# Mamba's dt bias as a row of ones in the product, softplus in three ScalarE steps, and new orders of turns

## The reference

```python
def mamba_block(x, Wi, cw, cb, Wx, Wdt, bdt, Alog, Dp, Wo):
    xz = x @ Wi.T
    xs, z = jnp.split(xz, 2, axis=-1)          # 256 inner features each
    ...                                        # causal convolution of xs, 4 taps
    u = jax.nn.silu(conv + cb)
    xdbl = u @ Wx.T                            # 8 + 16 + 16 columns
    dt, Bc, Cc = jnp.split(xdbl, [DT_RANK, DT_RANK + D_STATE], axis=-1)
    dt = jax.nn.softplus(dt @ Wdt.T + bdt)
    A = -jnp.exp(Alog)
    # h = exp(dt A) h + dt B u ; y = C h, over 256 steps, 16 states
    y = y + u * Dp
    y = y * jax.nn.silu(z)
    return y @ Wo.T
for i in range(NUM_LAYERS):
    x = mamba_block(layer_norm(x, ln_w[i], ln_b[i]), ...) + x
```

## Time and profile before

| | |
|---|---|
| median of 3 runs | 1870.89 us (1869.44 to 1872.04) |
| the profiled execution | 1878.92 us |
| its span, first to last instruction | 1877.1 us |
| busy: TensorE, VectorE, ScalarE, GpSimd | 80%, 81%, 72%, 63% |
| mean granted clock of TensorE | 0.877 |

### The profile page before, as it was taken

The page is one execution under the profiler, slowest core; times in us unless marked ns, Lnnn a source line. Parts: engine busy times, 40 slices in busy tenths (PEclk is TensorE's granted clock), DMA queues, the critical chain, the costliest instruction groups (busy, mean ns, idle before and its releaser), DMA issues. The chain is left out here.

```text
span 1877.1 us, 27473 instructions
## 1 busy us (share of the span) xinstructions
PE 1493.4 (80%) x9417; PEld 1056.8 (56%) x9417; DVE 1519.8 (81%) x2326; ACT 1342.7 (72%) x2733; POOL 1186.2 (63%) x999
## 2 busy tenths in 40 slices
...
PEclk9677767678899999777799999989999997989998
...
GB/s 191 1 69 74 123 9 92 108 68 92 128 113 119 124 102 108 71 64 23 68 120 130 105 130 137 79 111 46 119 133 137 140 102 69 65 32 79 115 21 6
DMA packets 84585, 170.10 MB, mean 91 GB/s; under 512 B 9440, under 2 KB 14944, under 8 KB 84064
## 3 DMA queue, kind: packets, MB, share of 16 engines
...
## 5 line engine op out<-in xcount | busy, mean ns | idle before, releaser
L1058 POOL TENSOR_TENSOR m<-m 128x1024 f32<-128x1024 f32 x256 | 765.8, 2996 | 191.5 <-DVE m L1049 191.3
L1049 DVE TENSOR_TENSOR_SCAN m<-m,dtuB 128x1024 f32<-128x1024 f32 x256 | 584.4, 2283 | 30.5 <-ACT m L1025 10.6
L1025 ACT ACTIVATE m<-m,Aneg 128x255 f32<-128x255 f32 x1024 | 429.9, 497 | 28.0 <-DMA m<-m 18.4
L1041 DVE TENSOR_TENSOR dtuB<-m 128x1024 f32<-128x1024 f32 x256 | 373.0, 1457 | 9.8 <-DMA m<-m 2.4
L1464 PE MATMUL ps<-o 128*128 128x256 f32 x512 | 151.3, 407 | 24.9 <-DVE X L1408 12.8
L1077 PE MATMUL ps<-m,w_const 128*32 128x256 f32 x2048 | 158.3, 439 | 12.5 <-POOL m L1058 12.5
L1431 ACT ACTIVATE o<-ps,w_mo 128x256 f32<-128x256 f32 x256 | 114.3, 470 | 61.1 <-PE ps L1464 59.7
L364 POOL TENSOR_TENSOR o<-o,mhalf 128x2 f32<-128x2 f32 x64 | 20.5, 320 | 204.9 <-DVE o L358 204.7
L964 PE MATMUL ps<-m,wc 128*128 128x256 f32 x512 | 135.2, 423 | 8.6 <-ACT m L385 8.6
L1472 PE MATMUL ps<-o 128*128 128x128 f32 x1024 | 130.8, 281 | 5.6 <-ACT o L1431 5.5
L1472 PEld LDWEIGHTS ps<-o 128*128 128x128 f32 x1024 | 123.8, 195 | 16.2 <-issue 10.3
...
## 6 DMA issues: line engine op xcount, KB each, us to landing
m<-m SPq DMA_DIRECT2D x256, 256.0 KB, 4.8
...
o<-in_mox SPq DMA_DIRECT2D x128, 256.0 KB, 3.0
...
```

The source lines that it names most:

```text
L1025: op = e.activation(dA[at % NA][:, j, 1:CH], R[q][:, h * CH + 1:h * CH + CH], ACT.Exp, scale=Aneg[:, l, 4 * g + j:4 * g + j + 1])
L1041: e.tensor_tensor(dtuB[:, :, :], bc(R[q][:, (2 + h) * CH:(3 + h) * CH].unsqueeze(1), 4, CH), Br[k % 2], ALU.mult).then_inc(S.dve, n.tick(f ...
L1049: e.tensor_tensor_scan(flat(G[at % NG]), flat(dA[at % NA]), flat(dtuB[:, :, :]), 0.0, ALU.mult, ALU.add).then_inc(S.dve, n.tick(f"s{g}"))
L1058: e.tensor_tensor(G[at % NG], G[at % NG], Cr[k % 2], ALU.mult).then_inc(S.pool, n.tick(f"c{g}"))
```

## The change

The bias of dt goes into the product: W_x gets a 41st column of zeros, so that row 40 of its result is zero; the copy to `v.xd` becomes an Identity step with a bias column that is 1 in row 40 and 0 elsewhere; and row 40 of the W_dt operand holds the bias. The product in PSUM is then v itself. Abs reads it from there, the Ln step writes to SBUF, and VectorE's L858 takes the maximum from PSUM and adds the SBUF part.

```diff
-MB, NMB = cols([("win", 512), ("wx", 2, 40), ("wdt", 256), ("wout", 2, 128),
-                ("cb", 2), ("bdt", 2), ("alog", 8, 4), ("dp", 2), ("lnw", 1), ("lnb", 1)])
+MB, NMB = cols([("win", 512), ("wx", 2, 41), ("wdt", 256), ("wout", 2, 128),
+                ("cb", 2), ("one", 1), ("alog", 8, 4), ("dp", 2), ("lnw", 1), ("lnb", 1)])
...
 ORDER = {
     "sp":
-        "uf3s8f3s8f3s8f3s8f3s8f3s8f3s8f3s8f2sa2s2fs4asa5fafa2s2bsbsbs4f2b2fbfsbs3bs4b3a3f3s2as2as4a4f3s3as2asa2sb3sa3f3sb"
+        "uf3s8f3s8f3s8f3s8f3s8f3s8f3s8f2s4fs4f2sa2s2fs4asa6f2b2asas4fs2bsb3f3s5b2s3b3a3f3s2as4as2a2faf2as4a2sasbsabsba3f3"
...
# Front.dve
-                e.scalar_tensor_tensor(v.dt, v.dt, 0.0, halves_of(b), ALU.max, ALU.add).then_inc(F.dve, n.tick("dt"))
+                e.scalar_tensor_tensor(v.dt, halves_of(b), 0.0, v.dtu, ALU.max, ALU.add).then_inc(F.dve, n.tick("dt"))
...
# Front.act
-                e.copy(v.xd[0:40, :], b[0:40, 0:CH]).then_inc(F.act, n.tick("xd"))
+                e.activation(v.xd[0:41, :], b[0:41, 0:CH], ACT.Identity, bias=m("one", l)[0:41, 0:1]).then_inc(F.act, n.tick("xd"))
                 yield
                 e.wait_ge(F.pe, n.pe("wd"))
-                for h in range(2):
-                    e.activation(v.dt[:, h, :], b[:, h * CH:h * CH + CH], ACT.Identity,
-                                 bias=m("bdt", l)[:, h:h + 1]).then_inc(F.act, n.tick(f"v{h}"))
-                e.wait_ge(F.act, n.act("v1"))
-                e.activation(v.dtu, v.dt, ACT.Abs).then_inc(F.act, n.tick("ab"))
+                e.activation(v.dtu, halves_of(b), ACT.Abs).then_inc(F.act, n.tick("ab"))
...
-                e.activation(halves_of(b), v.dtu, ACT.Ln, bias=1.0).then_inc(F.act, n.tick("ln"))
+                e.activation(v.dtu, v.dtu, ACT.Ln, bias=1.0).then_inc(F.act, n.tick("ln"))
...
# Front.pe
-                    op = e.matmul(b[0:40, 0:CH], m("wx", l)[:, h, :], v.u[:, h, :], start=h == 0, stop=h == 1)
+                    op = e.matmul(b[0:41, 0:CH], m("wx", l)[:, h, :], v.u[:, h, :], start=h == 0, stop=h == 1)
...
-                    op = e.matmul(b[:, h * CH:h * CH + CH], m("wdt", l)[0:40, h * 128:h * 128 + 128], v.xd[0:40, :],
+                    op = e.matmul(b[:, h * CH:h * CH + CH], m("wdt", l)[0:41, h * 128:h * 128 + 128], v.xd[0:41, :],
...
# packing of the weights
-        xs = wx[:, bc + list(range(8))]
+        xs = np.concatenate([wx[:, bc + list(range(8))], np.zeros((256, 1), np.float32)], axis=1)
+        one = np.zeros((128, 1), np.float32)
+        one[40] = 1.0
         wdt[32:40] = g("L1_attn_W_dt")[l].T
+        wdt[40] = g("L1_attn_b_dt")[l]
```

More of the change, by code:

```diff
@@ L214 @@
+        "sbs4b2s3b5f3bsbs3bs4b2f3s8f2sas3fs4f2bs3fs4a3sfafsafs4asas2a4f3s7b3sb3fbf2s3bs5b3a3f2afa2sas6a2sa5b3afaf2s5bs3b7"
+        "f2b2s3bs2bfbs3f3sa4s5a2sa2sa4f3s8b5f3bsbs2bs2asb2s2ba2ba2faf2s5as3a2f3s8a3ba2b2af3b2s6bsasb5f3b2s3bs2bs3bf3s8a12"
+        "b10ab2a10b2ababa2b3ab9ab",
     "pe":
-        "a9ua2ua3ba2ba7bab2ab8ab2ab2ab5a3bab2a2f2b3faf2bab2abasa4b2a3fa2f2af2sa2bab2abab2asb2fab4sfabfsaf2bfsb2fsab2af2af3"
-        "b2sa3bab2a2safbabasa5fafbfa2fsfa6sa2fasaf2b2sfafafb2sb2fa2fsfbf2bfb2sb8sb2afsb4fsf3bfbsfsa2bf3asf2b2asfa2sbababa2"
@@ new lines @@
+        "a9uaua4ba2ba7b2a2b10ababab6a3bab2a2bfbfbf2afasbab3a4b2a5fafaf3sba6b2sbfbab2sb3abfbfbsfaf2b3sbfa2sf2baf2bfb2a2ba2"
+        "sba2sbafa2ba4fafsabf3a2sa3ba4sfa2b2afsfsa2f3bsb2f2a2f2bfsbfsb7sb6fb2sbsf2abf3sbsfba3f2bfbsf2asa3b2fba4bfbfbafaf2"
+        "ba2s2a2b2asbfsa2ba2f2abfa2fbafsa3ba3b2a2sa2babfasbab2f2sabfbfafba3ba5ba2sb2a2bfaba2bsabfafb2fbfsbfb2a2ba2basba2b"
+        "afa6babfa4bfa2fa3fabfbs2bab7ab2sb6abfasbab2a2fbfafsfabfb3sfb4fa2b6fb4fa2fa2fsbsaba2b2a2sabfb2a2b2a3safa2fabf2baf"
+        "asa2b2ababa5ba3sab2afb3afafb2faf2s2b12sb2fb2a3babf2b2fa3safsfab3a2sa2b2fafasbfafaf2asb3aba3sabfba2bsfb2fabfafa2b"
@@ new lines @@
+        "b3a2bab2",
+    "dve":
+        "au2a7ubu3b7a11ba2fb2fb3a7b5fb2fs3fs2bsbs2bs4b2sb2fs8fs2f2as8a2sfafa2fsfs4as4asa2safbs2a2s2b2s3ba2ba2saba2fs2f2s6"
+        "bsb2sb2fs8fs2f2s6as2a2sb2f2a2babsb2fbfbs6bs6fas8fs4f2s7a2f2afasfs2bfs12fsb2a2b3sfsbaf2babafbasbs8bfbs7a2fsbf2sas"
+        "a2sbsabs2bs4fs8fs2as2f2a2sb2s4absb2afsabs3fsaf2s11afsbasfs2bfbafs2abs4as3a2sbfs2abas2asbsa2fsbs3f2s2bs2as2as3afa3"
+        "bfa2f2sas3bs2asbs2asasb2s2a3ba3ba2fabs2b2as2asas3a2fb2f2bsa4sa3fb5sbs5b2fbs3b6sb2abs2fba2fb2fa2fasb2s4ab2sb5fs7a2"
+        "safaf2s2a2s6as2as2bfs2babsabsb2s2fs2f2s2bs5b2sbabfas4b2sa3fsaf2sb4s8fs7faf2a2s3absbas4b2asbsfbas4as4fsfsas2fsabs3"
+        "b2a2bfs2bs2a2sbfa2bsf2as2a2bs4bs4abafa6bas3abs2ab2as2fbf2bfa8bsasb2sasasafs3a2sbsb2sa2sasasb3sb3fs2f2bfba2s2bs4b4"
+        "ab2asasb2asbsfsb3s3b2sfs2f2sbs2basbsa2s2bsfs2as3fs2as2f2s5bsbas3fbafb2fbfs3as10fs4as2fbs2bf2bas4bs2bs3fsbas2bs2f"
+        "sf2sbas6bs4afabsbasfas2baf2sasabsbs5a3ba3ba2fabs2b2asasas2a6ba2bfabsfb2saba2sb2sa2bs2ba2babas6b9s2abab2sa3fabfb5"
+        "a4b2abab3a2bab2ab2ab2aba2ba2b2aba2b3aba2b3a6b3a2b2ab4a4b2aba4b3ab3ab3ab3ab",
@@ new lines @@
+    "act":
+        "a3ua4ua2ua2uba2ba2ba5bab4ab5aba2b6a3bafba2fbfbfbf2afab3a2sbasbafsbasasafafsasf2af2asa2bas2ab2s2bsb4sfbfsbasf3b2f"
+        "absasf2sasbsfafsbfbfba2bas4a2babsa2sasa2fafsabfbf2a2fsa2sasbasas2a2s2b2af2s2faf3ab3s2f2as3af2bfsfsb3s2b3s2b4sbs2"
+        "b3f2s2faf2bfs2bfasf2s3fabfsf2sasba2sbab2a2fas2f2bsa2fb2fa2fsfs2a2bs2ba2bs2a4fafaba2fb2fsafs2afasab2asasb2asasas2"
+        "bab3f2asbfabfbfbsabfa4babsa2bsabsbasba2fasfbs2fbfbfsbfba2ba2sba3sasa3bafbsa2fa2s2bfafa3fsfsba2b3sb3abs2ab4sabasb2"
+        "asabfbfsafbafsf2b2asb2sbfba2sbfb3sbs2b2afba2fafab2fas2ba2bs2ba2basab2sa2bafb2sa2safafsabfb2fafsafab2aba2ba3ba2sa"
+        "sbabsb2abfbfasfsbabfbfaf2b2sbsbsbsb2sb2sb3a2bafb2fs2bfa3bfasf2sabsabsa2s2b2a2sfs2fa2bf2a2fsfsb3asasa3sababsbfbfb"
+        "abasfafasafsafb2as2abab2as2asbfababfs2afbfabafbab2asa3b2fasbaba2sabsbsabasb2a2s2aba2bafba2fsa2bsf2ba2fba2fba3bas"
+        "b3sbsabab2sbab3f2asbfab2fabsbafbafb2abab2abs3b2a2b4ab2asababs2afsf2abfafbfasfa2b2asabsba2saba2babs2a5b3afa2bfbfs2"
+        "fba2bfa2bsasfa3sfabababsabab2sasasbabsbafbfsbfafbfsafasb2s2ab2sab2s2ab2fsfsa2sfbfabafa2bfab3ab2sa2sfsfabas2fba2f"
+        "bfs2bfbsb2sba2bs2a2bs2a2f2basabfbfbfsbfb2sb2a2b2sa2bs2ab3s2fabfb3s2fbfba2bfsfb5a2sb2sb2asb2sbabf2sasa2safbafba2f2"
+        "bsa2bsb2a3basabsab2abasa4sb2aba4baba2sba2bsba4b2sb2aba2ba6ba2baba2babababab5ababa3b2a2b4a2ba2b4a2b2a2b3a2ba2ba4b2"
+        "a4b2ab3ab3abab2a2ba2b5abab7ab4ab4a3b2aba2bab4a2b2a2ba3b2ab4a2b2ab3a2bab2",
```

48 lines of the change are left out of this document (10 added, 38 removed).

## The result

The changed kernel takes 1893.22 us (median of 4 runs, 1886.66 to 1899.67); on the same chip the kernel before took 1871.47. The ratio is 1.0101, 95% interval 1.0072 to 1.0131: slower by 19 us by the ratio (22 between the medians) where I had forecast 9 less.

A forecast was written before the change was run, and what follows sets the result against it. VectorE was taken to bound the scan stretch (88% busy, 181 us idle), TensorE the end. The terms -5.5 - 2 + 1.5 - 2 - 2 = -10 us gave 1861, shaved to 1862.0 us; range 1848 to 1876.

The forecast's parts named there:

- Part 1, softplus: ScalarE's softplus steps: 0.78 us less per unit, 25 us over 32 units, of which 5.5 us on the path.
- reading (a): VectorE's ten waits for the last softplus step L934, 9.6 us in all: shortening them gives 5.3 us.
- further -2 for ScalarE's later work: Scan stretch: the freed 0.78 us lets ScalarE's next work start sooner; -2 us, bounds 0 and -6.
- Part 2, table loads: ScalarE's activation tables: 192 loads instead of 188, +5.1 us on its queue, +1.5 us on the path.
- Part 3, fronts: ScalarE's queue between L385 and Ln holds 15.3 us instead of 16.9 per unit; -2 us, at most 3.
- Part 3, covers: VectorE work between a unit's last scan and L838: gained 9.6 us, lost 7.3; net -2, bounds -16 and +7.
- the four gains: Units 7, 24, 17 and 26 get more cover before L838: 3.4 + 2.5 + 2.3 + 1.4 = 9.6 us.
- Part 3, "everything else that moved": Experts, attention and tail in the new order: 0 us, bounds -5 and +5.
- The tail: Behind the last L838: TensorE's, same work, unchanged at 213 us; a move over 5 us would show the forecast wrong.
- The slower one: VectorE before L838 in units 4, 11, 29 and 1: thinner covers cost 7.3 us; +8, 1879 us; chance 0.16.
- sign of error: TensorE's granted clock falling from 0.9 to 0.7 at about 520 to 750 us and from 990 on would show it wrong.

The follow-up runs named there:

- code_only: The changed kernel's new softplus with the order of turns of the kernel before; 1865.15 us, ratio 0.9971 to the kernel before.

## Why the prediction was wrong

**Part 1, softplus: right.** It had -5.5 us on the path; 5.4 were measured with the old order (interval 1 to 10 us), and the wait for the last step fell by 5.0 in code_only where reading (a) had 5.3. The further -2 for ScalarE's later work cannot be seen apart from it. The durations came out as worked out, and ScalarE's busy time fell by 17 us instead of 20, and in code_only, without the four loads, by 24 instead of 25.

**Part 2, table loads: not measured alone.** The count was right, 192 against 188. The rows after show again no time around a load, 0.02 us ahead of it and 0.01 behind. The Trainium skill (ScalarE: Activation LUTs, What ACT_TABLE_LOAD costs) has a drain of about 1.4 us there for a switch of sets; here the measurement decides.

**Part 3, fronts: wrong in sign.** I had counted what ScalarE's queue holds between xT and Ln, 1.6 us less, and taken -2. The wait for the last softplus step came to 13.1 us instead of going under 4. With the old code the new order has it at 26.5. ScalarE's own queue did hold less between xT and Ln (17.6 us a unit before, 16.0 now in the traces), so what makes Ln late lies ahead of it, most likely in when its inputs come through TensorE; that queue I had not counted, and no run isolates it.

**Part 3, covers: the sign was right, the places only in part, and it was worth nothing.** Waits before L838 fell from 15.9 to 4.3 us, 3.1 of the 11.6 already with the old order (12.8 in code_only). Unit 7 has none now, and unit 4 has 1.3 instead of the 3.0 forecast. But I had taken a thin cover for a wait: of the four gains, those of units 24 and 17 (2.5 and 2.3 us) had no wait before L838 to lose, and units 16 and 25, which I had not named, lost 2.8 and 2.0. VectorE's idle time in the scan stretch stayed at 181 us, so the 11.6 us came back as waits elsewhere.

**Part 3, "everything else that moved": the step that failed.** It said 0, bounds -5 and +5. Measured, the order costs 24 us with the new code. I had followed the new turns on VectorE and ScalarE only. In the two places looked into, units 0 to 3 and unit 24, the loss comes through TensorE. In the first the order puts more of the other lines' matmuls between two hand-overs of the scan (6.8 us at an equal clock), and in both the granted clock is lower with it (0.70 against 0.78, and 0.82 against 0.94 in code_only). That VectorE is fuller over the stretch (88% against TensorE's 80%) hid this: there VectorE waits for a TensorE that has its lower level for 86 of 144 and 24 of 67 us, and being nearly full elsewhere it does not make up for it.

**The tail: just outside.** The text said it would be wrong if the tail moved by more than 5 us. It moved by 7 in the profile, and by 5 to 8 in every profile with the new tail against most with the old one; "the same work up to four of 588 instructions" says nothing on its order.

**The rivals.** The slower one had the right sign and the wrong place: its price was to be paid before L838, where time was gained. I had also given as a sign of error that the clock falls between 520 and 750 us and from 990 on. It did not, with 0.98 and (to 1800 us) 0.94 both before and after; it fell in the first 400 us, where it was low already (0.74 to 0.71), and in unit 24 (0.92 to 0.82). The missing rival was "more of TensorE's work between two hand-overs". A part of it could have been counted in the order, 554 instead of 532 TensorE instructions between the first L838 and the fourth, 4 to 6 us of its time; the fall of the clock there could not.
